# LayerNorm statistics of the first sublayer: one ScalarE pass and one VectorE sum in place of four ScalarE passes

## The reference

```python
def _layernorm(x, axis=-1, eps=1e-5):
    m = jnp.mean(x, axis=axis, keepdims=True)
    v = jnp.var(x, axis=axis, keepdims=True)
    return (x - m) / jnp.sqrt(v + eps)
...
x = x + _L0_attn_a_ref(_layernorm(x, axis=-1), ...)   # long convolution along the width 4096, kernel from an S4 state space
x = x + _L0_ffn_ref(_layernorm(x, axis=-1), ...)      # routed scales, product with sign(weight), bias
x = x + _L0_attn_b_ref(_layernorm(x, axis=-1), ...)   # QKV product, attention over the 2 sequences of a token, output product
x = x + _L0_ffn_ref(_layernorm(x, axis=-1), ...)      # the same FFN again
```

## Time and profile before

| | us |
|---|---|
| median of 3 runs | 8632.06 |
| lowest, highest | 8598.03, 9041.34 |
| the profiled execution: time | 8632.06 |
| the profiled execution: span of the slowest core (core 3) | 8630.5 |
| the profiled execution: span of the fastest core | 8580.4 |

### The profile page before, as it was taken

The page is one execution under the profiler, slowest core; times in us unless marked ns, Lnnn a source line. Parts: engine busy times, 40 slices in busy tenths (PEclk is TensorE's granted clock), DMA queues, the critical chain, the costliest instruction groups (busy, mean ns, idle before and its releaser), DMA issues.

```text
span 8630.5 us, 73907 instructions; the slowest of 8 cores (8580.4 to 8630.5 us)
## 1 busy us (share of the span) xinstructions
PE 5638.8 (65%) x25740; PEld 2507.7 (29%) x25740; DVE 1665.1 (19%) x3446; ACT 1287.3 (15%) x2600; POOL 335.4 (4%) x444
## 2 busy tenths in 40 slices
PE   2402343377588757885787668874788578767886
PEld 0101111133233323332333233332333233323333
DVE  3212010002310223022211231022202221223102
ACT  0211000011211111111111121112111111212111
POOL 0000000000001000100010000100010001000010
PEclk9855666687688777877788778886888778777887
DMA  1299999975166534645266516652565446452664
GB/s 42 64 273 208 163 163 160 161 206 189 35 216 231 177 117 156 234 166 185 103 229 215 195 36 217 228 189 72 176 232 193 140 153 228 165 195 78 229 228 157
DMA packets 355795, 1468.29 MB, mean 170 GB/s; under 512 B 18840, under 2 KB 18841, under 8 KB 343001
## 3 DMA queue, kind: packets, MB, share of 16 engines
q1 hardware_dynamic: 307658, 1211.68, 41.7%
q0 software_dynamic: 38560, 218.31, 12.8%
q10 hardware_dynamic: 9216, 33.56, 1.3%
HBM read 1480.33 MB, written 151.13 MB: 189 GB/s over the span
## 4 chain that ended last, share of the span: by engine, by line
PE 62%; DVE 13%; DMA 7%; another core or an unknown queue 6%; ACT 6%; issue 5%; POOL 1%; DVEq 1%; SPq 0%; ACTq 0%; POOLq 0%
PE PS L586 48%; PE PS L711 6%; PE PS L666 5%; DMA oscbf<-wffnT 3%; DVE res L826 2%; DVE tr L824 2%; DVE ln_bf L652 2%; DVE actT L785 2%; ACT qkvsb L864 1%; DVE tr L722 1%; DMA res<-x_in 1%; PE PS L802 1%; ACT oscbf L806 1%; PE PS L780 1%
## 5 line engine op out<-in xcount | busy, mean ns | idle before, releaser
L586 PE MATMUL PS<-wbuf,actT 128*128 128x512 bf16 x18432 | 4275.8, 394 | 794.1 <-DMA wbuf<-qkv_bf 349.1
L586 PEld LDWEIGHTS PS<-wbuf,actT 128*128 128x128 bf16 x18432 | 1848.6, 101 | 3215.6 <-issue 1222.8
L666 PE MATMUL PS<-ident_sb,ln_bf 128*128 128x128 bf16 x2048 | 384.5, 269 | 1455.9 <-DVE ln_bf L652 1352.2
L666 PEld LDWEIGHTS PS<-ident_sb,ln_bf 128*128 128x128 bf16 x2048 | 209.0, 107 | 1644.9 <-issue 1563.2
L603 ACT ACTIVATE ln_bf<-res 128x2048 bf16<-128x2048 f32 x96 | 183.3, 1910 | 2765.1 <-DVE res L826 1254.1
L824 DVE TENSOR_TENSOR tr<-PS,oscbf 128x512 f32<-128x512 f32 x256 | 177.0, 692 | 2043.0 <-PE PS L586 2018.3
L711 PE MATMUL PS<-ttoep,actT 128*128 128x512 bf16 (+3 forms) x2304 | 492.7, 379 | 99.4 <-DVE res L725 94.8
L880 DVE TENSOR_REDUCE alph<-prodb 128x3 f32<-128x384 f32 (+1 forms) x96 | 49.0, 510 | 1883.0 <-POOL prodb L876 1883.0
L675 ACT COPY actT<-PS 128x128 bf16<-128x128 bf16 x1280 | 340.7, 266 | 463.4 <-PE PS L666 404.1
L864 ACT CAST qkvsb<-PS 128x512 bf16<-128x512 f32 x192 | 112.6, 587 | 1580.2 <-PE PS L586 1565.7
L670 DVE COPY actT<-PS 128x128 bf16<-128x128 bf16 x1280 | 287.7, 225 | 308.4 <-PE PS L666 237.3
(11 more groups left out here) (159 smaller groups left out, 1690.3 us busy)
## 6 DMA issues: line engine op xcount, KB each, us to landing
wbuf<-ffn_bf SPq DMA_DIRECT2D x256, 2048.0 KB, 8.7
wbuf<-qkv_bf SPq DMA_DIRECT2D x192, 2048.0 KB, 8.5
wbuf<-proj_bf SPq DMA_DIRECT2D x128, 2048.0 KB, 8.7
qkv_bf<-wqkvT POOLq DMA_DIRECT2D x3, 16384.0 KB, 393.7
res<-x_in POOLq DMA_DIRECT2D x16, 2048.0 KB, 14.6
qkvsb<-wffnT POOLq DMA_DIRECT2D x32, 1024.0 KB, 9.0
oscbf<-wffnT POOLq DMA_DIRECT2D x32, 1024.0 KB, 9.4
ffn_bf<-oscbf ACTq DMA_DIRECT2D x64, 512.0 KB, 6.5
```

The source lines that it names most:

```text
L586: e.matmul(psv(bb, g), blocks_actT[bb][:, c * 128:(c + 1) * 128], wbuf[bi][:, cc * COLW + g * 512:cc * COLW + (g + 1) * 512], start=(c == ...
L666: pe_n = pe(lambda e, v=view, sap=src_fn(c): e.transpose(v, sap, ident_sb[:]), inc=True)
```

## The change

In the way of `ln_stats` that the first sublayer takes, the four ScalarE passes over 128x2048 go. In their place ScalarE does one Square over the whole 128x4096, with the sum of the squares in the second column of this block's part of `stat`, and VectorE sums the block itself by one `reduce_sum` over 128x4096 into the first column. The two read the same block and don't wait for each other. The two VectorE additions of the halves are now in the other way only, since here there are no halves; in that way they keep their place behind the wait for ScalarE, so the last three sublayers issue the same instructions as before.

```diff
             if hv is None:
-                for h in (0, 1):
-                    cols = slice(h * 2048, (h + 1) * 2048)
-                    act(lambda e, cols=cols, o=o, h=h: e.activation(
-                        ln_bf[:, 0:2048], x[:, cols], AF.Copy,
-                        accum_out=stat[:, o + 2 * h:o + 2 * h + 1]))
-                    hvv = act(lambda e, cols=cols, o=o, h=h: e.activation(
-                        ln_bf[:, 0:2048], x[:, cols], AF.Square,
-                        accum_out=stat[:, o + 2 * h + 1:o + 2 * h + 2]), inc=True)
+                hvv = act(lambda e, o=o: e.activation(
+                    ln_bf[:], x[:], AF.Square,
+                    accum_out=stat[:, o + 1:o + 2]), inc=True)
+                dve(lambda e, o=o: e.reduce_sum(stat[:, o:o + 1], x[:], axis=AX.X))
             else:
                 hvv = max(hv.values())
+                P.wait("vector", s_act, hvv)
+                dve(lambda e: e.tensor_add(stat[:, o:o + 1], stat[:, o:o + 1], stat[:, o + 2:o + 3]))
+                dve(lambda e: e.tensor_add(stat[:, o + 1:o + 2], stat[:, o + 1:o + 2], stat[:, o + 3:o + 4]))
             P.wait("vector", s_act, hvv)
-            dve(lambda e: e.tensor_add(stat[:, o:o + 1], stat[:, o:o + 1], stat[:, o + 2:o + 3]))
-            dve(lambda e: e.tensor_add(stat[:, o + 1:o + 2], stat[:, o + 1:o + 2], stat[:, o + 3:o + 4]))
             dve(lambda e: e.tensor_scalar(stat[:, o + 4:o + 5], stat[:, o:o + 1], 1.0 / D, None, ALU.mult))
```

## The result

| | before | after |
|---|---|---|
| lowest of 12 runs, us | 8598.03 | 8531.92 |
| median of 12 runs, us | 8868.74 | 8733.92 |
| ratio, 95% interval | | 0.9919 (0.989 to 0.9947) |
| the profiled execution, us | 8632.06 | 8539.04 |

In 7 of the 12 runs before and in 6 of the 12 after, the cores of one die or of both had a lower granted clock and took longer, which lifts both medians by some 200 to 250 us; the ratio leaves these runs out, and the middle of the others is 8618.6 us before and 8540.0 after. So the change makes the kernel 0.8% faster, some 70 us (0.0081 x 8632; the interval allows 46 to 95), within the 2% that I called about what a measurement tells from no change.

A forecast was written before the change was run, and what follows sets the result against it. Bound by ScalarE's four uncovered statistics passes per call at the tile seam, 8.98 us; gains of 4.40 and 4.61 us by block make 9.01 a tile, 72 over eight: 8632 - 72 = 8560 us, range 8515 to 8605.

The forecast's parts named there:

- The stretch: From first statistics pass to the mean in the first sublayer: 8.98 us before, gains of 4.40 and 4.61 by block.
- The prices: Extrapolated instruction times over 4096 columns: VectorE's reduce 4.44 us from line 880's slope, ScalarE's Square 3615 ns.
- The rival of the long reduce that loses its pace: Reduce over 4096 columns at the reciprocal's pace, 26.2 us: 278 us slower in all, 8910 us; chance 0.03.
- the one in which it runs at line 652's pace: Reduce takes 2.7 us, so ScalarE ends last in the stretch: gain 80 us, 8552 us; chance 0.07.
- Who ends last: In the new stretch VectorE's reduce, 4.44 us, ends after ScalarE's 3.72; ScalarE's result comes some 0.3 us earlier.
- The two readers: VectorE and ScalarE reading one block don't disturb each other, nothing added; taking turns completely would leave a 12 us gain.
- The first tile: Gain ahead of the weights' preparation counted in full; 9 us lost if the shared memory gives nothing back.
- the rival of the shared memory: End of the first tile's weight preparation set by shared memory, so only seven tiles gain 63 us: 8569 us; chance 0.10.
- the 20 us of the rival: Shift puts more of the convolution's starts at TensorE's low clock, costing 20 us: 8580 us; chance 0.10.
- The prediction's sign of being wrong: Convolution groups longer than 16.73 us for 80 matmuls in the profile after would show the forecast wrong.
- The sum: Profiled execution 8632.06 us, also the median of the runs, minus 72 us gives 8560 us.
- How the numbers follow: Forecast weighted 0.70; range 8515 to 8605 us, using two runs 34 us apart; within 2% has 0.95.

The follow-up runs named there:

- e8_after_again: The changed kernel as it is, run again as base for later runs: 8562.6 us, ratio to the kernel before 0.9911.
- e2_halves: Kernel before with its halves kept, but the sums of x moved to two VectorE reduces beside ScalarE's two Squares: 8566.6 us, ratio to before 0.990.
- e1_merge: Kernel before with both sums still on ScalarE, each as one pass over 128x4096: 8609.8 us, 32 us under before.
- e4_square_twice: The changed kernel with the Square run twice in each call: 8613.2 us, ratio to the kernel before 0.995.
- e6_own_load: The changed kernel with each block waiting only for its own load instead of both: 8517.8 us, ratio to the kernel before 0.9863.

## Why the prediction was right, and where it was wrong

- **The stretch.** Predicted 4.58 us in block 0, and 4.37 us from ScalarE's start in block 1 (2208.71 - 2204.34); measured 4.49 and 4.32. The gain in it is 4.49 + 4.66 = 9.15 us a tile, in place of 9.01.
- **The prices.** The reduce was extrapolated from 256 and 384 columns to 4096: 4.44 us, measured 4.42; for 2048 the same slope gives 2.30, measured 2.29. The Square: 3.615 us, measured 3.617. The rival of the long reduce that loses its pace falls with this, as does the one in which it runs at line 652's pace. The Trainium skill ("VectorE: DVE Perf Modes", Rules for kernel authors) expects the reduce at the lowest rate and advises against it on a hot path. The trace agrees with a low rate, 1.04 ns a column where line 652 has 0.66 (the reciprocal of line 352 has 6.4), but the reduce was still worth using, since ScalarE's passes had been one after the other on the same path. (Where the prediction calls the case with line 652's pace the second rival, it is the first of its list.)
- **Who ends last.** VectorE, by the doubled reduce (all of it is paid, stretch and tiles) and the doubled Square (0.6 us are free).
- **The two readers.** No disturbance: 4.42 us with and without the Square beside it.
- **The first tile.** A delay put in passes on, which speaks against the rival of the shared memory. Whether the 9 us won there reach the end isn't shown: what I didn't foresee is how far the end of this tile is scattered over cores, by 30 to 40 us, half of the whole gain. The middle of the cores issues its first store at 2147 us before, at 2130 after and at 2140 in e8_after_again, 17 and 7 us earlier.
- **93 us between the profiled executions, not 72.** The first tile isn't the reason. Each slowest core compared with the other, its first tile ends 2154.4 - 2143.5 = 10.9 us earlier and its seven tiles are 82 us shorter (6468.0 on core 3 before, 6385.7 on core 5 after). Of these 82, 17 are core 3's own: its tiles before took 923.3 us, where core 5 had 921.0 and the middle of the cores is no longer. Why core 3 was slower no run tells.
- **The clock.** The first group of 80 convolution matmuls took 17.0 us on average before and 16.7 after over the tiles and cores, as the chain has them. In e2_halves, which shifts them by nearly as much, it is 17.1 again, and in e1_merge, which shifts them least, 16.7. So it moves by some tenths of a microsecond either way, no sign of the 20 us of the rival. The prediction's sign of being wrong, groups longer than 16.73 us, was badly set: that is a single row, and under the average of the kernel before.
- **The time.** 8560 us was forecast for the median, and the range of 8515 to 8605 missed it: the median came out at 8733.92. The mechanism and the 72 us held; what failed is the term that they were taken from, the 8632 of "The sum", and with it the range in "How the numbers follow". I took 8632.06 for the level of the kernel before because it was the median of three runs; over twelve runs that median is 8868.74. And I took the spread from two of the three, 8598.03 and 8632.06, and gave no weight to the third, 9041.34, which stood in the same table. The median then fell by 135 us, nearly twice the 72, which is chance: it depends on how many of the twelve are long. The difference that the trace does tell, 72 us or a ratio of 0.9917, was measured as 0.9919 (0.989 to 0.9947), and the runs that the ratio compares lie within the range.

What stays open: e1_merge, e2_halves and e4_square_twice came out 7 to 15 us better than their stretches make them (32 for 21, 75 for 60, 28 for 21 us). For the first two it doesn't lie in the seven later tiles, which are 10.9 and 55.1 us shorter where the stretches make 18 and 52. The scatter of the first tile, and of the totals they are compared with, is large enough for it, but no run here isolates it.

## What to carry to other kernels

Two sums over the same freshly loaded block, at a place where everything waits, belong on two engines; the price of the slower one is the whole price, and it can be read from a short instruction of the same kind by its slope. When the chain shows such a stretch, look at what stands right before it too: here the wait for both loads was worth two thirds of the change itself, and storing and loading by halves more. And state a difference from a trace as a difference: one profiled execution shows nothing of the level of a median, and when one of three runs stands 5% above the others, that run belongs in the range.

## What the runs showed of the hardware that I had not expected

- The sum of one row of 4096 has the slope of rows of 128 within half a percent: 2286 ns for 2048 columns (e2_halves) and 4420 for 4096, 1.042 ns a column, against 1.047 in the earlier trace rows.
- At the seam the load of block 0, issued while the store of block 1 is on its way and followed by the load of block 1, takes 14.4 to 14.6 us to land, and that of block 1 12.0 (2 MB each). So a load issued 7.4 us earlier is there only some 5 us earlier.
- Between two dependent column instructions of VectorE, usually 0.1 us apart, there is now and then a gap of 0.46 to 0.48 us, once in the changed kernel's second tile (line 630 after 629), in e6_own_load after the reduce instead. What it waits for the profile doesn't show.
